# First attention: products of values in pairs in periods 0 and 2, output products in pairs in periods 1 and 3, rows turned in float16

## The reference

```python
def _L0_attn_ref(x, emb_weight, qkv_w, o_w):
    ...
    qkv = x @ qkv_w.T
    qkv = qkv.reshape(B, S, 3, N_HEAD, HEAD_DIM)
    ...
    scale = HEAD_DIM ** (-0.5)
    scores = jnp.einsum('bhqd,bhkd->bhqk', q, k) * scale + bias
    attn = jax.nn.softmax(scores, axis=-1)
    a = jnp.einsum('bhqk,bhkd->bhqd', attn, v)
    a = a.transpose(0, 2, 1, 3).reshape(B, S, N_HEAD * HEAD_DIM)
    return a @ o_w.T
...
x = _layernorm(x + _L0_attn_ref(x, L0_attn_emb_weight, L0_attn_qkv_w, L0_attn_o_w), axis=-1)
x = _layernorm(x + _L0_xattn_ref(x, ctx_512, ...), axis=-1)
x = _layernorm(x + _L0_ffn_ref(x, ...), axis=-1)
```

## Time and profile before

| what | us |
| --- | --- |
| median of 3 runs | 1291.46 |
| lowest and highest | 1283.61, 1292.37 |
| the profiled execution: time | 1287.09 |
| the profiled execution: span, first to last instruction | 1285.4 |
| PE busy in the span | 1183.4 (92%) |
| DVE, ACT, POOL busy | 924.5, 820.9, 498.6 |
| first attention, roughly | 25 to 568 |

### The profile page before, as it was taken

The page is one execution under the profiler, slowest core; times in us unless marked ns, Lnnn a source line. Parts: engine busy times, 40 slices in busy tenths (PEclk is TensorE's granted clock), DMA queues, the critical chain, the costliest instruction groups (busy, mean ns, idle before and its releaser), DMA issues.

```text
span 1285.4 us, 25128 instructions
## 1 busy us (share of the span) xinstructions
PE 1183.4 (92%) x8870; PEld 542.9 (42%) x8870; DVE 924.5 (72%) x2376; ACT 820.9 (64%) x1577; POOL 498.6 (39%) x519
## 2 busy tenths in 40 slices
PE   6799999999999999868899988888888999999998
PEld 2344444444444444334333233322332366666666
DVE  3777777777777777767788787778876567656564
ACT  3566666666666666634677766676666777667663
POOL 0167878888777778914212111131111131000000
PEclk9999999999999999988999999999999899999999
DMA  7634333322233332021121221122100523232300
GB/s 221 172 98 117 96 93 84 111 80 80 80 84 83 84 82 81 13 71 42 46 81 43 65 61 42 43 56 69 42 26 1 197 89 109 75 139 97 118 17 17
DMA packets 82483, 103.00 MB, mean 80 GB/s; under 512 B 12627, under 2 KB 74067, under 8 KB 82327
## 3 DMA queue, kind: packets, MB, share of 16 engines
q1 hardware_dynamic: 81174, 100.87, 26.8%
q10 hardware_dynamic: 160, 0.39, 0.1%
q0 software_dynamic: 1024, 0.13, 0.1%
HBM read 65.37 MB, written 10.68 MB: 59 GB/s over the span
## 4 chain that ended last, share of the span: by engine, by line
PE 75%; DVE 14%; ACT 4%; issue 4%; DMA 1%; POOL 1%; ACTq 0%; SPq 0%; DVEq 0%; POOLq 0%
PE a_s L1299 10%; PE a_o L464 9%; DVE a_mx L1607 8%; PE a_m L1285 7%; PE a_o L1218 6%; PE a_a L409 6%; PE a_s L454 5%; PE a_s L455 4%; PE a_m L1173 4%; PE a_e L504 3%; PE a_a L419 3%; PE a_m L432 3%; PE a_a L166 3%; PE a_s L1200 3%; PE a_s L1285 2%
## 5 line engine op out<-in xcount | busy, mean ns | idle before, releaser
L1607 DVE TENSOR_REDUCE a_mx<-a_m 128x1 f32<-128x512 f32 (+3 forms) x512 | 271.5, 583 | 80.4 <-PE a_m L1173 71.3
L1432 ACT ACTIVATE a_pt<-a_s 128x512 f32<-128x512 f32 (+3 forms) x512 | 235.0, 515 | 115.4 <-PE a_s L1200 112.9
L635 ACT ACTIVATE a_pt<-a_s 128x512 f32<-128x512 f32 x256 | 149.5, 597 | 167.4 <-DVE a_s L762 139.6
L753 DVE CUSTOM_DVE_ANT_0 a_junk<-a_m,a_rtile 128x512 f16<-128x512 f32 x256 | 167.3, 687 | 0.7 <-issue 0.7
L844 POOL TENSOR_TENSOR a_ps<-a_ps,a_pt 128x512 f32<-128x512 f32 x128 | 159.8, 1271 | 0.7 <-ACT a_pt L635 0.7
L464 PE MATMUL a_o<-a_pt,a_v 128*64 128x512 f32 x512 | 139.8, 624 | 2.6 <-DVE a_a L767 2.5
L1853 POOL TENSOR_SCALAR_AFFINE_SELECT a_pt<-a_pt 128x512 f32<-128x512 f32 x64 | 40.6, 635 | 229.4 <-ACT a_pt L1432 229.4
L762 DVE TENSOR_TENSOR a_s<-a_s,a_near 128x218 f32<-128x218 f32 (+1 forms) x256 | 107.9, 433 | 13.8 <-PE a_s L455 10.6
L454 PE MATMUL a_s<-a_q,a_k 128*128 128x512 f16 x256 | 99.3, 388 | 7.1 <-ACT a_pt L635 6.1
L742 DVE TENSOR_TENSOR a_nat<-a_a,a_nat 128x512 f16<-128x512 f32 x64 | 44.3, 692 | 84.2 <-ACT a_nat L610 84.2
L844 POOL TENSOR_TENSOR a_ps<-a_pt 128x512 f32<-128x512 f32 x64 | 80.1, 1273 | 57.0 <-ACT a_pt L635 57.0
(11 more groups left out here) (295 smaller groups left out, 2622.8 us busy)
## 6 DMA issues: line engine op xcount, KB each, us to landing
a_rtile<-lines SPq DMA_DIRECT2D x32, 448.0 KB, 3.9
a_q<-a_nat SPq DMA_DIRECT2D x192, 64.0 KB
a_k<-a_nat SPq DMA_DIRECT2D x192, 64.0 KB
a_vy<-in_Wa SPq DMA_DIRECT2D x12, 1024.0 KB, 4.9
a_vy<-in_Wb SPq DMA_DIRECT2D x12, 1024.0 KB, 7.4
a_qk<-halves SPq DMA_DIRECT2D x40, 128.0 KB, 2.7
halves<-a_held SPq DMA_DIRECT2D x16, 256.0 KB, 2.3
halves<-a_held SPq DMA_DIRECT2D x32, 128.0 KB, 2.4
```

The costliest lines, as they stand in the source:

```text
L635: act.activation(pt[:, n % RING, ::-1], bank_s[j % 2][:, :], ACT.Exp, scale=SC1 / QS).then_inc(sm["act_s"], 1)
L753: dve.tensor_tensor_reduce(junk[h][:, :], bank_m[h][:, :], rtile[:, u % 3, h, qb * P:qb * P + S], 1.0, -3e38, ALU.add, ALU.max, mx[u % 2][ ...
L1432: act.activation(pt[g % 4][:, h, first:], bank_s[(32 * u + j) % 3][:, first:], ACT.Exp, scale=SC2 / QS).then_inc(sm["act_s"], 1)
L1607: dve.tensor_reduce(mx[u % 2][:, qb, to:to + 1], bank_m[j % 3][:, 0:keys], AX.X, ALU.max).then_inc(sm["dve_b"], 1)
```

## The change

- `pv` is issued two blocks at a time: blocks 0 and 1 in period 2, blocks 2 and 3 in period 0. The exponentials stay where they were, so block 1's product now stands in the period of its exponentials, and so does block 3's.
- `project_out` is issued two blocks at a time, in periods 1 (blocks 0 and 1) and 3 (blocks 2 and 3). The two share a bank, half each (`out_banks`). Its waits, and those of `weigh` and `add_out`, are for pairs; `weigh` and `add_out` run one period later than before, the last of a unit in the next slot's period 0.
- A new DVE instruction `negative` (128 x 8) scales the maxima by -1/MAXROW into a float16 tile `mx16`; `rows` is then a float16 product with a float16 identity in the place of a float32 transpose, and ACT's copy has no scale. The float16 identity is loaded at the start (32 KB).
- ACT: `high_o` from period 2 to the head of period 1, `high_sum` behind the second exponential of period 2, `rows` behind `weigh` in period 0.
- In the last two units the waits around the banks follow the pairs.

```diff
@@ out_banks
-            return bank_s if u >= LAST and qb % 2 == 1 else bank_e
+            half = slice(qb % 2 * C, (qb % 2 + 1) * C)
+            return [bank[:, half] for bank in (bank_s if u >= LAST and qb >= 2 else bank_e)]
@@ tensor
             def rows(u):
-                pe.wait_ge(sm["dve_b"], 8 * u + 8)
+                pe.wait_ge(sm["dve_n"], u + 1)
...
-                    mm = pe.transpose(bank_a[0:2, qb * P:(qb + 1) * P], mx[u % 2][:, qb, :], ident[:, :])
+                    mm = pe.matmul(bank_a[0:2, qb * P:(qb + 1) * P], mx16[:, qb, :], second.ident16[:, :], start=True, stop=True)
@@ project_out
-                elif n > 0:
+                elif n > 0 and n % 2 == 0:
                     pe.wait_ge(sm["dve_x"], n)
                     pe.wait_ge(sm["act_x"], n)
@@ tensor, the loop
-                    if 0 <= t - 4 < UNITS:
+                    if i % 2 == 1 and 0 <= t - 4 < UNITS:
+                        project_out(t - 4, i - 1)
                         project_out(t - 4, i)
-                    u = t - 2 if i > 1 else t - 3
-                    if 0 <= u < UNITS:
+                    u = t - 2 if i == 2 else t - 3
+                    if i % 2 == 0 and 0 <= u < UNITS:
                         pv(u, (i + 2) % 4)
+                        pv(u, (i + 2) % 4 + 1)
@@ scalar, the loop
                     u = t - 2 if i > 0 else t - 3
-                    if i == 2 and 0 <= t - 3 < UNITS:
+                    if i == 1 and 0 <= t - 3 < UNITS:
                         high_o(t - 3)
                     if 0 <= u < UNITS:
                         exponential(u, (i + 3) % 4 * 2)
...
+                    if 0 <= u < UNITS:
+                        exponential(u, (i + 3) % 4 * 2 + 1)
                     if i == 2 and 0 <= t - 3 < UNITS:
                         high_sum(t - 3, 0)
                         high_sum(t - 3, 1)
-                    if 0 <= u < UNITS:
-                        exponential(u, (i + 3) % 4 * 2 + 1)
+                    if i == 0 and 0 <= t - 5 < LAST:
+                        weigh(t - 5, 3)
                     if i == 0 and 0 <= t - 2 < UNITS:
                         rows(t - 2)
-                    if 0 <= t - 4 < LAST:
-                        weigh(t - 4, i)
+                    if i > 0 and 0 <= t - 4 < LAST:
+                        weigh(t - 4, i - 1)
@@ vector
+            def negative(u):
+                dve.wait_ge(sm["dve_b"], 8 * u + 8)
+                if u > 0:
+                    dve.wait_ge(sm["pe_rows"], u)
+                dve.tensor_scalar(mx16[:, :, :], mx[u % 2][:, :, :], -1 / MAXROW, None, ALU.mult).then_inc(sm["dve_n"], 1)
...
                     u = t - 2 if i > 0 else t - 3
+                    if i == 0 and 0 <= t - 5 < UNITS:
+                        add_out(t - 5, 3)
                     if i == 2 and 0 <= t - 3 < UNITS:
                         low_o(t - 3)
...
                     if 0 <= t - 1 < UNITS:
                         maximum(t - 1, i)
-                    if 0 <= t - 4 < UNITS:
+                        if i == NT - 1:
+                            negative(t - 1)
+                    if i > 0 and 0 <= t - 4 < UNITS:
+                        add_out(t - 4, i - 1)
+                    if i == 3 and t - 4 == UNITS - 1:
                         add_out(t - 4, i)
```

More of the change, by code:

```diff
@@ L227, in attention_1 @@
                                        "pool_lo pe_sum dve_r pe_o act_o dve_o pe_e0 pe_e1 dve_x act_x pool_x "
-                                       "cst2 w2_in w2_hi w2_lo ld_ctx bias pe_br act_br dve_br dve_e1 dve_lo")
+                                       "cst2 w2_in w2_hi w2_lo ld_ctx bias pe_br act_br dve_br dve_e1 dve_lo dve_n ld_id16")
         moved = [sm[f"moved{c}"] for c in range(3)]
@@ L245, in attention_1 @@
         mx = [sb(f"mx{p}", [P, NT, 2]) for p in range(2)]
+        mx16 = sb("mx16", [P, NT, 2], F16)
         pt = sb("pt", [P, RING, S])
@@ L325, in sync @@
                 sp.dma_start(k2[c][D1:ROWS1, :, :], io["select1"]).then_inc(sm["cst"], DMA)
+            sp.dma_start(second.ident16[:, :], io["ident16"]).then_inc(sm["ld_id16"], DMA)
             for b in range(1, B):
@@ L366, in sync @@
                 if u == 4:
-                    for dst, name in ((second.tri_q[:, :, :], "tri_q"), (second.identm[:, :, :], "identm"),
-                                      (second.ident16[:, :], "ident16"), (second.braw[:, :], "b2")):
+                    for dst, name in ((second.tri_q[:, :, :], "tri_q"), (second.identm[:, :, :], "identm"), (second.braw[:, :], "b2")):
                         sp.dma_start(dst, io[name]).then_inc(sm["cst2"], DMA)
@@ L476, in sums @@
                 else:
-                    pe.wait_ge(sm["dve_x"], 4 * u if u <= LAST else 4 * u - 1)
+                    pe.wait_ge(sm["dve_x"], 4 * u if u <= LAST else 4 * u - 2)
                 for h in range(2):
@@ L492, in project_out @@
                     pe.wait_ge(sm["dve_r"], u + 1)
-                if n == 4 * LAST + 1:
+                if n == 4 * LAST + 2:
                     pe.wait_ge(sm["act_s"], 8 * UNITS)
-                elif n > 4 * LAST + 1:
-                    pe.wait_ge(sm["dve_e1"], n - 1 - 4 * LAST)
-                elif n > 0:
+                elif n > 4 * LAST + 2 and n % 2 == 0:
+                    pe.wait_ge(sm["dve_e1"], n - 2 - 4 * LAST)
+                elif n > 0 and n % 2 == 0:
                     pe.wait_ge(sm["dve_x"], n)
@@ L503, in project_out @@
                         hd = slice(h * D1, (h + 1) * D1)
-                        mm = pe.matmul(out_banks(u, qb)[h][:, 0:C], a16[u % 2][hd, i, tok], w[hd, u % PAIRS, :], start=n == 0,
+                        mm = pe.matmul(out_banks(u, qb)[h], a16[u % 2][hd, i, tok], w[hd, u % PAIRS, :], start=n == 0,
                                        stop=n == 2)
@@ L622, in rows @@
                 for h in range(2):
-                    act.activation(q2[u % 3][D1:D1 + 2, h, :], bank_a[0:2, :], ACT.Copy, scale=-1 / MAXROW
+                    act.activation(q2[u % 3][D1:D1 + 2, h, :], bank_a[0:2, :], ACT.Copy
                                    ).then_inc(sm["act_rows"], 1)
@@ L655, in weigh @@
                     act.wait_ge(sm["pool_x"], n - 3)
-                act.activation(part[n % 4][:, :], bank_e[1][:, 0:C], ACT.Identity, scale=r[u % 2][:, 1, qb:qb + 1]
+                act.activation(part[n % 4][:, :], out_banks(u, qb)[1], ACT.Identity, scale=r[u % 2][:, 1, qb:qb + 1]
                                ).then_inc(sm["act_x"], 1)
@@ L859, in gpsimd @@
                 for i in range(NT):
-                    u = t - 4 if i > 0 else t - 5
+                    u = t - 4 if i > 1 else t - 5
                     if 0 <= u < LAST:
-                        add_out(u, (i + 3) % 4)
+                        add_out(u, (i + 2) % 4)
                     if i == 3 and 0 <= t - 2 < UNITS:
```

16 lines of the change are left out of this document (9 added, 7 removed).

## The result

The changed kernel takes 1426.39 us (median of 4 runs, 1424.55 to 1427.41) where the kernel before takes 1288.03 on the same chip (median of 4 runs). The ratio is 1.107, with a 95% interval from 1.102 to 1.112: slower by a tenth. The profiled execution took 1427.41, its span is 1425.7, 140.3 more than before.

What follows compares the result with a forecast made beforehand. PE's work was taken to bound the first attention's slots; 28 slots times 2.86 (80 us) plus 3 us for slots 2 and 3 took 1287.1 to 1370, or 1374.5 for a median; range 1335 to 1410.

Steps and rivals of the forecast that it cites:

- one mechanism: First attention: PE waits in period 2 for exponential 3; 2.5 to 3.4 us more in a slot; chance 0.72.
- The chain from score 0 to the end of exponential 3: DVE and ACT steps in a slot, each waiting on the one before; unchanged by the edit, 9.3 us.
- The bias of score 3: DVE in period 2: reached no earlier than 8.1 us after score 0, else the prediction is wrong.
- PE's pause: Period 2: block 1's values' product, wanted at about 6.8, may go at 9.3; PE waits 2.5 us.
- `sums` behind the second `add_out`: Period 0: `sums` waits for block 3's `add_out`, which writes the same bank; PE waits 0.55 us.
- Score 0 behind ACT's rows: Slot's end: ACT's `rows` behind `weigh` ends at 18.4, PE is done at 18.2; score 0 waits 0.2 us.
- The slot that these make: First attention, score 0 to next score 0: 18.4 us in place of 15.54, 2.9 us more.
- slower still, by the clock: Rival: PE's pause lowers its clock, about 1.5 us a slot; in each of 28 slots 42 us more, 1417; chance 0.10.
- a sign of being wrong: The prediction called itself wrong if the clock's row is below 0.95 in the middle.
- `negative`: 0.15 forecast: New DVE instruction before `rows`: above nothing, not above 0.21 us plus a semaphore's way; taken as 0.15 us.
- The float16 rows: 0.22 forecast: PE in period 0: `rows` as float16 products costs 0.22 us in place of 0.44, saving 0.22 a slot.
- Start and end: 3 and 0 forecast: Slots 2 and 3 cost 1.5 us more each, 3 us; last four slots 0 with 5 either side; early load 0.

Runs made afterwards that it cites:

- the kernel with the reduction: The changed kernel with `negative` written as a reduction over an axis of one in place of the multiplication with a scalar: 1414.09 us, ratio 1.103.
- The run with one pause filled and rows in float32: The changed kernel with float32 rows, no `negative`, and nine products with zeros in PE's pause of period 2: 1373.91 us, ratio 1.069 to the kernel before.
- filling the first: The changed kernel with nine products with zeros in PE's pause of period 2: 1427.11 us, ratio 1.111 to the kernel before.
- the kernel with 416 instructions more on PE: The changed kernel with products with zeros: nine in period 2's pause, three ahead of `rows`, two ahead of `sums`: 1400.4 us, ratio 1.089 to the kernel before.

## Why the prediction was wrong, and what of it held

It said slower, by one mechanism, and the mechanism is there. The time, 1426.4, lies 52 above the forecast and 16 above the range, because the clock was put at next to nothing.

**What held.** The chain from score 0 to the end of exponential 3: forecast 9.3, and the product behind it starts at 9.25. The bias of score 3: 8.1 and 8.00. PE's pause: 2.5 and 2.25. `sums` behind the second `add_out`: 0.55 and 0.48. Score 0 behind ACT's rows: 0.2 and 0.17. The slot that these make: 18.4; 18.47 is measured in the kernel with the reduction, in the slots where the clock holds. So the 80 us forecast for 28 slots are there: 28 times (18.47 - 15.54) = 82. That the values' pair makes most of it, its edit alone (1.090) and the change without it (1.032) show. The run with one pause filled and rows in float32, in which the clock holds, comes out at 1373.9 beside the forecast of 1374.5; that they are so near is partly luck, since that kernel has no `negative`, slots of 18.24, and a start and an end of its own.

**The step that failed: the clock.** The sum has no term for it. I had it as a rival, "slower still, by the clock", with a chance of 0.10, against it that "the time in front of the pause is dense with work". That reason was wrong: in the changed kernel the clock fell in 23 of 28 slots, and the row from 200 to 300 us is at 0.90, under the 0.95 that the prediction itself names as a sign of being wrong. The price was right: 1.5 a slot, and 20.08 - 18.47 = 1.6 is measured. In 23 slots that is 37 us. The range's top, 1410, was meant to take in such a clock, but 1374.5 and 23 times 1.5 fill it up and leave nothing for the terms below. Two stretches of the earlier trace rows, one with a fall and one without, could not tell how often it would come. The passage of the Trainium skill that the prediction names at this rival ("TensorE: Matmul & The Clock Gate", section "HAM oscillation") tells of a loop with longer waits than these 2.25 us; that waits as short as this bring falls, this trace shows. I looked at one pause for the clock, and there were two places: filling the first left 22 falls behind the second.

**`negative`: 0.15 forecast.** Its own length is right, 0.17. Its upper bound, 0.21 and a semaphore, was none, since it came from another form of instruction: the reciprocal of the earlier trace rows runs at 316.10 beside an addition on POOL and takes 0.21 all the same.

```profile
315.78 0.72 POOL L856 TENSOR_TENSOR x_acc<-x_acc,a_part 128x256 f32<-128x256 f32 x1
```

Held by POOL `negative` is 0.79, in 10 of the 28 slots; 20.46 beside 20.08 where the clock falls, 19.08 beside 18.47 where it doesn't, so 4 to 6 us. The trace of before had a hint of it, POOL at 80% busy.

**The float16 rows: 0.22 forecast, 0.03 measured.** By the skill's rule in "Perfetto Trace Analysis", section "Transposes", the gain would not be had, and the trace agrees in that it isn't; the argument by which I set the rule aside took a price from other float16 products. It cost nothing in the sum, since `rows` waits for DVE anyway.

**Start and end: 3 and 0 forecast, 8.4 and 5.2 measured.** Slot 4 is reached at 85.90 and not 77.55, and from slot 32 to the end it is 773.2 and not 768.0. Of the 8.4, 1.6 are there when slot 2 starts, at 45.43 for 43.87, and that start varies from 42.9 to 45.6 in the traces. The other 6.8 are slots 2 and 3, for which I had taken 3: in slot 2 PE waits 5.38 us for the last exponential of period 2, and the clock is at 0.50 behind it. The end can't be put down to the change: in the fifteen traces it takes 765.3 to 775.2, and 774.0 and 766.5 in two kernels that differ only in the place of one output block.

**The sum, mended:** 82 for the order, 37 for the falls, 5 for the long `negative`, 8 for what the two slots with weight splits have beyond the others, less 4.8 that before had of such stalls, is 127; measured is 566.58 - 439.87 = 126.7. With 8.4 and 5.2 it makes the 140.3. The rival as I had priced it, 1417, is 9 short, near to what the start and the end have beyond the forecast; in between, terms that it lacked and its falls in all slots happen to cancel.

## What to carry to other kernels

When products are put in pairs on an engine that is full, ask for each when its last input is there: the pair is as late as the later of the two, and everything behind it on the engine pays. A pause that a change brings has a second price, the clock's; work it out for every place where the engine waits, short waits around tiny instructions too, and give it a term of the sum where the trace already shows a fall. For a new instruction on DVE ask what POOL does at that moment and which form doesn't meet it.

## What the runs showed of the hardware that I had not expected

- A pause of 2.25 us in a slot of 18 to 20 brings the clock from 1.00 to 0.50 (18 falls in 28 slots), and waits of 0.68 and 0.48 us around four and sixteen tiny products do it as well (6 falls, and 22 with the pause filled). It stays there for some 3.4 us and costs 1.4 to 1.6 us. Five slots with the same waits have no fall, and what decides it is not shown.
- Products with zeros keep it at 1.00: the kernel with 416 instructions more on PE is 26 us faster, 24 by the ratios.
- A `tensor_scalar` of 128 x 8 takes 0.17 us, or until POOL's addition ends (0.79, up to 1.31); a reduction of the same size takes 0.16 in the midst of that addition.
- Four float32 transposes of 128 x 2 and four float16 products in their place cost the same within 0.03 us, gaps around them included.
